# A transformer encoder on one core: where the attention probabilities are divided by their sums

## The reference

```python
for l in range(L):                                   # L = 4
    y = _layer_norm(h, ln_a[l, 0], ln_b[l, 0])
    qkv = jnp.einsum('bsd,tde->tbse', y, attn_w[l, :3]) + attn_b[l, :3][:, None, None, :]
    ...
    scores = jnp.einsum('bhqd,bhkd->bhqk', q, k) * inv_sqrt_dk
    p = jax.nn.softmax(scores, axis=-1)
    o = jnp.einsum('bhqk,bhkd->bhqd', p, v).transpose(0, 2, 1, 3).reshape(b, s, D)
    h = h + o @ attn_w[l, 3] + attn_b[l, 3]
    y = _layer_norm(h, ln_a[l, 1], ln_b[l, 1])
    h = h + jax.nn.relu(y @ w1[l] + b1[l]) @ w2[l] + b2[l]
```

## Time and profile before

| what | us |
|---|---|
| median of 3 runs | 2325.65 |
| the profiled execution's own time | 2324.32 |
| its span in the trace | 2322.4 |
| TensorE busy | 2114.2 (91%) |
| VectorE busy | 1298.6 (56%) |
| ScalarE busy | 1023.5 (44%) |

### The profile page before, as it was taken

One profiled execution on the slowest core, in us unless ns is written; L12 is line 12 of the kernel. 1 busy time (PEld: TensorE's weight loads), 2 busy tenths in 40 slices (PEclk: granted clock), 3 DMA queues, 4 the chain that ended last, 5 costly groups with the idle time before them and its releaser, 6 DMA issues. The chain is left out here.

```text
span 2322.4 us, 43354 instructions
## 1 busy us (share of the span) xinstructions
PE 2114.2 (91%) x16462; PEld 1701.4 (73%) x16462; DVE 1298.6 (56%) x3287; ACT 1023.5 (44%) x3502; POOL 148.0 (6%) x183
## 2 busy tenths in 40 slices
PE   4899999999999999999999878898998699999990
PEld 3688878887878888887888657777776588877770
DVE  3676767676766667676766346555545654122222
ACT  3566565666565666656565224343434211111110
POOL 4000000000000000000000000000000000400005
PEclk8999999999999999999999989999999699999995
DMA  5000000100003000000000000000000500144436
GB/s 165 1 2 1 1 2 5 59 2 1 1 2 135 2 1 1 2 1 2 1 1 2 1 18 1 1 0 0 0 1 2 203 0 3 41 134 147 141 104 120
DMA packets 28825, 75.87 MB, mean 33 GB/s; under 512 B 5853, under 2 KB 19133, under 8 KB 25202
## 3 DMA queue, kind: packets, MB, share of 16 engines
q1 hardware_dynamic: 17010, 58.77, 7.4%
q0 software_dynamic: 3840, 7.44, 2.0%
q10 hardware_dynamic: 7808, 7.34, 0.9%
HBM read 59.81 MB, written 16.78 MB: 33 GB/s over the span
## 5 line engine op out<-in xcount | busy, mean ns | idle before, releaser
L417 ACT ACTIVATE probs<-bank,nmax 128x256 f32<-128x256 f32 x1024 | 474.0, 478 | 414.5 <-DVE nmax L562 414.5
L562 DVE TENSOR_REDUCE nmax<-bank 128x2 f32<-128x512 f32 x512 | 318.0, 684 | 237.7 <-PE bank L296 237.7
L309 PE MATMUL bank<-ident,probs 128*128 128x128 f32 x2048 | 272.1, 276 | 4.1 <-DVE pts L570 4.1
L309 PEld LDWEIGHTS bank<-ident,probs 128*128 128x128 f32 x2048 | 232.7, 141 | 38.8 <-DVE pts L570 21.7
L341 PE MATMUL bank<-yT,weights 128*128 128x256 f32 x1024 | 249.1, 387 | 2.0 <-ACT yT L404 1.1
L353 PE MATMUL bank<-weights,aT 128*128 128x256 f32 x1024 | 232.7, 381 | 2.5 <-DVE aT L618 1.2
L417 ACT ACTIVATION_READ_ACCUMULATOR probs<-bank,nmax 128x1 f32 x1024 | 215.4, 210 | 0.0
L341 PEld LDWEIGHTS bank<-yT,weights 128*128 128x128 f32 x1024 | 185.4, 191 | 38.9 <-ACT aT L440 11.6
L353 PEld LDWEIGHTS bank<-weights,aT 128*128 128x128 f32 x1024 | 189.9, 190 | 26.3 <-DVE aT L618 1.5
L570 DVE COPY pts<-bank 128x512 f32<-128x512 f32 x256 | 173.5, 678 | 39.2 <-PE bank L309 39.2
L999 ACT ACTIVATE w_probs<-w_bank,w_nmax 128x144 f32<-128x144 f32 x256 | 113.2, 523 | 155.3 <-DVE w_nmax L1155 155.3
(11 more groups left out here) (198 smaller groups left out, 2912.6 us busy)
## 6 DMA issues: line engine op xcount, KB each, us to landing
we<-in_experts SPq DMA_DIRECT2D x16, 1024.0 KB, 5.0
weights<-in_wtok SPq DMA_DIRECT2D x4, 2048.0 KB, 11.2
we<-in_experts SPq DMA_DIRECT2D x16, 512.0 KB, 4.0
expert_rows<-zeros SPq DMA_DIRECT2D x10, 512.0 KB
weights<-in_wtok SPq DMA_DIRECT2D x4, 1024.0 KB, 4.9
xrows<-expert_rows SPq DMA_DIRECT2D x16, 256.0 KB, 4.1
expert_outs<-ye ACTq DMA_DIRECT2D x16, 256.0 KB, 4.0
wqkv<-in_wqkv SPq DMA_DIRECT2D x1, 3072.0 KB, 18.3
```

The costliest lines, as they stand in the source:

```text
L309: last = pe.transpose(g[:, (NT * x + kb) * P:(NT * x + kb + 1) * P], p[:, x, kb * P:(kb + 1) * P], ident[:])
L417: last = nc.scalar.activation(probs[u % 8][:, x, :], g[:, x * S:(x + 1) * S], ACT.Exp, bias=nmax[j % 2][:, col:col + 1], accum_out=rsum[j ...
L562: nc.vector.tensor_reduce(nmax[j % 2][:, col:col + 2], g[:].rearrange("p (x s) -> p x s", x=2), AX.X, ALU.max, negate=True).then_inc(s_max, 1)
```

## The change

The probabilities are divided by their sums before they are transposed. Of the four tiles of a group VectorE inverts the sums (128 x 8) and multiplies tiles 0 and 1 in place (`low_probs`), and ScalarE multiplies tiles 2 and 3 in place, a 128 x 256 activation for each head (`high_probs`). Both stand at the end of their engine's program for the group. `recips`, `r_T`, `r_out`, `o_norm` and their tiles are gone; the attention output is copied out of bank 6 by ScalarE (`o_out`), which stands at the start of group c = 1. `turn_probs` waits for the multiplied tile instead of the exponentials.

```diff
@@ TensorE
-            def r_T(j):
-                if real(j):
-                    transposed((j, "rT"), rb[:].rearrange("p i n d -> p i (n d)"), s_rb, j + 1)
...
                 g = acquire(pe, (j, "pt", 4 * c + n))
-                evacuated(pe, (j, "S", 4 * c + n))
+                pe.wait_ge(s_low if n < 2 else s_high, 2 * (GROUPS * j + c) + n % 2 + 1)
...
                     turn_probs(jp, cp, 0)
                     turn_probs(jp, cp, 1)
-                    if c == 0:
-                        r_T(j - 1)
@@ ScalarE
+            def high_probs(j, c):
+                if not real(j):
+                    return
+                act.wait_ge(s_rinv, GROUPS * j + c + 1)
+                for n in (2, 3):
+                    p = probs[(4 * c + n) % 8]
+                    for x in range(2):
+                        last = nc.scalar.activation(p[:, x, :], p[:, x, :], ACT.Copy, scale=rinv[c % 2][:, 2 * n + x:2 * n + x + 1])
+                    last.then_inc(s_high, 1)
...
+                    if c == 1:
+                        o_out(j - 1)
                     exps(j, c, 0)
...
                     exps(j, c, 2)
-                    if c == 0:
-                        r_out(j - 1)
...
                         relu(j - 1, 0)
+                    high_probs(j, c)
@@ VectorE
+            def low_probs(j, c):
+                if not real(j):
+                    return
+                evacuated(dve, (j, "S", 4 * c + 3))
+                col = (c // 2) * H + 8 * (c % 2)
+                nc.vector.reciprocal(rinv[c % 2][:], rsum[j % 2][:, col:col + 8]).then_inc(s_rinv, 1)
+                dve.wait_ge(s_rinv, GROUPS * j + c + 1)
+                for n in (0, 1):
+                    p = probs[(4 * c + n) % 8]
+                    nc.vector.tensor_tensor(p[:], p[:], rinv[c % 2][:, 2 * n:2 * n + 2].rearrange("p (x s) -> p x s", s=1)
+                                            .to_broadcast((P, 2, S)), ALU.mult).then_inc(s_low, 1)
...
                     jp, cp = divmod(GROUPS * j + c - 1, GROUPS)
-                    if c == 0:
-                        recips(j - 1)
                     if c == 1:
                         fed_forward(j - 2, 0)
-                        o_norm(j - 1)
...
                         relu(j - 1, 3)
+                    low_probs(j, c)
```

More of the change, by code:

```diff
@@ L99, in embed_and_encoder @@
         rsum = [sb(f"rsum{x}", [P, NT * H]) for x in range(2)]
-        rinv = sb("rinv", [P, NT * H])
+        rinv = [sb(f"rinv{x}", [P, H // 2]) for x in range(2)]
         probs = [sb(f"probs{i}", [P, 2, S]) for i in range(8)]
         pts = [sb(f"pts{i}", [P, 2, NT, P]) for i in range(8)]
-        rb = sb("rb", [P, NT, H, DK])
-        rT = sb("rT", [P, KD, S])
         oT = sb("oT", [P, KD, S])
@@ L124, in embed_and_encoder @@
                 if c == 0:
-                    use((j, "v"), 7), use((j - 1, "rT"), 0), use((j - 2, "down", 0), 7)
+                    use((j, "v"), 7), use((j - 2, "down", 0), 7)
                 if c == 1:
@@ L146, in embed_and_encoder @@
         s_free = [sem(f"s_free{i}") for i in range(8)]
-        s_max, s_rb, s_half, s_step = sem("max_ready"), sem("rb_ready"), sem("half_ready"), sem("dve_step")
+        s_max, s_rinv, s_low, s_high = sem("max_ready"), sem("rinv_ready"), sem("low_probs"), sem("high_probs")
+        s_half, s_step = sem("half_ready"), sem("dve_step")
         s_yn, s_var, s_sd = ([sem(f"{n}{k}_ready") for k in (1, 2)] for n in ("yn", "var", "sd"))
@@ L426, in copy_pt, with o_out @@
                 release(nc.scalar.activation(pts[(4 * c + n) % 8][:], g[:].rearrange("p (x k s) -> p x k s", x=2, k=NT), ACT.Copy), u)
-            def r_out(j):
+            def o_out(j):
                 if not real(j):
                     return
-                g = take(act, (j, "rT"))
-                release(nc.scalar.activation(rT[:], g[:], ACT.Copy), (j, "rT"))
+                g = take(act, (j, "o"))
+                release(nc.scalar.activation(oT[:].rearrange("p k s -> p (k s)"), g[:], ACT.Copy), (j, "o"))
+            def high_probs(j, c):
[7 more added lines that the diff above has]
+                    last.then_inc(s_high, 1)
             def relu(j, i):
@@ L570, in copy_pt @@
                 release(nc.vector.tensor_copy(pts[(4 * c + n) % 8][:], g[:].rearrange("p (x k s) -> p x k s", x=2, k=NT)), u)
-            def recips(j):
+            def low_probs(j, c):
                 if not real(j):
                     return
[L575 to L587, removed]
+                evacuated(dve, (j, "S", 4 * c + 3))
[6 more added lines that the diff above has]
+                                            .to_broadcast((P, 2, S)), ALU.mult).then_inc(s_low, 1)
             def bias(j, row):
```

## The result

The changed kernel takes 2337.62 us (median of 5 runs, 2335.92 to 2340.44) against 2325.65: slower, ratio 1.0048 with a 95% interval of 1.0033 to 1.0062. A later measurement gave 1.0033 (1.0021 to 1.0045). The forecast was +8.0 us, 2333.5, in a range of 2326 to 2342. The profiled execution took 2337.62 us (span 2335.8).

What follows compares the result with a forecast made beforehand. TensorE, busy 1140 of 1162 us in the filled encoder, was taken as the bound. First groups 5.1, filling 1.5 and 0.5, and draining 0.9 summed to +8.0 us, forecast 2333.5, range 2326 to 2342.

Steps and rivals of the forecast that it cites:

- The transposes of the sums are worth nothing: First group, jobs 1 to 31: removing four transposes (0.52 us) counts 0, as TensorE waits for VectorE's copy anyway.
- The maxima of the next job are 0.17 late: First group, jobs 2 to 31: VectorE's new work delays row maxima and second transpose pair by 0.17, 5.1 us in all.
- upper end of 0.25: Largest delay per job allowed for the first group's row maxima: 30 x 0.25 = 7.5 us, if the multiplications don't overlap.
- The other groups cost nothing: Other three groups of a job: the multiplications fall in time in which VectorE waited for TensorE; counted as nothing.
- ScalarE's work is covered: Four new activations a group, 0.39 each, 1.6 us: exponentials 0.5 late, products with the values not delayed, nothing lost.
- the tightest place: Behind the third group on ScalarE: 0.2 us left before the fourth group's products wait for the copy of tile 3.
- Draining +0.9: End of the encoder: the last group's transposes wait for inversion and multiplications, +0.9 us.
- Filling +2.0: Job 0: new VectorE work ahead of the next maxima, +1.5 us; job 1: late output copy, together +0.5.
- three signs of being wrong: Pair within 4.0 us of the scores; multiplications at about 0.43; a new wait for ScalarE's copy before the fourth group's products.
- The chance of 0.53 for slower: Whole kernel: probability given to a slower result, beside 0.39 for the same and 0.08 for faster.

Runs made afterwards that it cites:

- the first try: Kernel before, with the output multiplication and the feed-forward addition of the second group in the other order on VectorE; one run, 2364.11 us.

## Why the prediction was right

- **The transposes of the sums are worth nothing.** Right in the filled jobs: 39.70 with and 39.69 without them. The whole run without them was 3.1 us shorter, in job 1, which the forecast for this term didn't have.
- **The maxima of the next job are 0.17 late.** Right in place and size: 0.16, gone when the work was moved. (Its upper end of 0.25 was too low by the forecast's own figures: two multiplications of 0.69 without overlap end 0.33 late. Nothing hung on it.) The choice of 0.69 for the multiplication, against 0.43 of a copy, decided this; it took 0.688, and the copy 0.43. The Trainium skill (VectorE: DVE Perf Modes, "The perf-mode tier table (the rule you actually need)") has a two-tensor operation in float32 go at one element a cycle where a float32 copy within SBUF goes at two; the trace agrees, with 0.688 for 512 columns.
- **The other groups cost nothing.** Wrong in one of them, the step "`o_norm` stood ahead of maxima that waited anyway: nothing for its going". Its going put two waits on the first maximum of the second group, one of which then became an instruction of its own: 0.07 in 30 jobs, 2.1 us. The account of the jobs is then 4.8 + 2.1 = 6.9 against 6.4 measured over 29 of them and a forecast of 5.1.
- **ScalarE's work is covered.** Right: 0.40 from start to start for the forecast 0.39, exponentials 0.54 late for 0.5, products on time. The copy of tile 3 was 0.23 late, not 0.34. The limit lay elsewhere, though: with eight shorter activations the fourth group lost 0.55 to the wait for bank 0, which the exponentials of tile 0 must leave, and nothing at the products, whose 0.2 of cover the forecast had worked out. The step that named the tightest place failed, at no cost to the sum.
- **Draining +0.9.** Right: 0.9 to 1.0 up to the encoder's last addition (43.05 before, 44.02 and 43.93 after), and gone with the work moved (42.93). The table's 1.1 to 1.2 holds some of the windowed stage's wait for a transfer.
- **Filling +2.0.** The two places are as forecast: the first maxima behind the normed rows of job 1 start 2.09 instead of 0.65 behind them, 1.44 for the forecast 1.5, and in job 1 the output copy ends 3.06 behind the next normed rows for the forecast 3.0. The sum isn't: from the rows to the scores of job 1 it is 1.8 to 3.1 us more, and job 1 itself, forecast +0.5, takes 0.1 to 0.3 less (40.95 and 40.81 against 41.00 and 41.09). The granted clock falls to its lower level at other places of job 1: it is 1.00 in the second group against 0.88 and 0.83, and 0.86 and 0.87 in the third against 0.95. The forecast had no term for the clock. In absolute time the share is -0.9 to +1.8, and not settled.
- **The sum.** 8.0 forecast; measured 12.0 (2337.62 and 2325.65) and 8.5 us (2361.82 and 2353.36). That the second is so near is in part luck: it holds 2.1 us that were not forecast and a filling that isn't known to have cost 2.0. None of the three signs of being wrong came: the pair starts 4.46 behind the scores and not within 4.0, the multiplications take 0.69, and no wait stands before the products of the fourth group. The chance of 0.53 for slower was on the right side, though little more than even, since the sum lay at the bound of what can be measured.

## What to carry to other kernels

Work that is removed from the busiest engine is worth its time only if that engine has no wait behind it: look for the smallest idle bracket after the place, and for what the removed work was covering. Where a chain over another engine sets that wait, new work on that engine belongs where it was idle by the trace, even if the program order looks natural otherwise. The gain is then taken by moving a longer piece into the hole.

## What the runs showed of the hardware

A second wait ahead of a VectorE instruction, on a semaphore long met, made it start 0.07 us later behind the wait that came last: 0.54 idle instead of 0.47, and 0.30 instead of 0.23, in each job. In the trace one of the two waits is then an instruction of its own (`EVENT_SEMAPHORE`, 0.021 us, 0.065 ahead of the row maximum). In the first try the maxima followed an instruction of VectorE without idle, and the 0.07 could not be read. In the second group of job 1 the same 80 matmuls kept TensorE busy for 7.25 and 7.96 us at a mean granted clock of 0.88 and 0.83 (the two traces of the kernel before) and for 6.40 us at 1.00 (without the sums' transposes). Two activations of 128 x 256 with a factor for each partition and SBUF as source started 0.40 apart, each 0.50 long, against 0.36 with PSUM as source.
